# Attention weights multiplied in every slot, and the scans' preparation moved between states

## Chip, core and metric

The program runs on one core of a Trainium2 chip. The metric is device time in microseconds (us), in the median of the runs. Five engines run side by side, each through its own instructions in program order: TensorE (PE) multiplies matrices, VectorE (DVE), ScalarE (ACT) and GpSimd (POOL) work on elements, SyncE (SP) issues DMAs. They wait for each other on semaphores alone.

## What is computed

Four layers, each `x = x + layer(norm(x))` on x of 4 x 96 x 56 x 56. Two kinds of stage matter here.

Layer 0 is attention with 3 heads per image over 3136 tokens, head size 16:

```python
attn = jnp.einsum('bhnd,bhmd->bhnm', q, k) * scale
attn = jax.nn.softmax(attn, axis=-1)
out = jnp.einsum('bhnm,bhmd->bhnd', attn, v)
```

Layers 1 and 3 scan the image along 8 and 4 directions with 192 channels and 16 states each. Layer 1:

```python
delta = jax.nn.softplus(dts + dt_projs_bias[None, :, :, None])
...
hc = hc * jnp.exp(d_t[..., None] * A[None]) + (d_t * u_t)[..., None] * B_t[:, :, None, :]
return (hc, jnp.einsum('bkdn,bkn->bkd', hc, C_t))
...
y = cross_merge(ys, h, w).reshape(b, DI, L)
```

Layer 3 is the same in outline; its states are `phi * cumsum(dbx / (phi + 1e-12))` with `phi = exp(-cumsum(dA))`. Layer 2 (a window attention) is not touched.

## The kernel before

**Attention** (205 to 2171 us). There are 12 heads `g` (4 images of 3), each in 7 passes `qc` of 448 queries, each pass in 13 slots `pi` of two key tiles of 128 (the last slot has one). In slot `n`, counted through all heads, PE writes two score tiles (L373, bf16) for ACT's exponential (L469, to `Pr[n % NPR]`), and between them one or two matmuls `maximum` (L310) of the next head, whose row maxima DVE reduces (L520). The weights times values, `pv(m)` (L335), are float32 matmuls, one for each key tile, into one of four strips of 32 columns of bank 4 (`j = t % 4`). `m` runs three slots behind `n`: in every second slot `pv(m - 1)` and `pv(m)` stand together, four matmuls, and the last slot of a pass stands alone. So a pass has 7 groups of them. After a pass `combine` (L342) adds the strips up, in the next slot. `NPR` is the number of buffers `Pr`; the exponential of slot `n` waits for `pv(n - NPR)`. `prep` spreads the preparation of the next image over the middle head of each of the first three images.

**Scans.** Layer 1 runs them twice (a pair of images each, 2387 to 6431 and 6746 to 10790 us), 8 directions of 7 tiles: 56 tiles. Layer 3 runs them twice (12224 to 14843 and 15428 to 18044 us) with 4 x 7 = 28 tiles, and there `ratio` is true. A tile is 448 positions in three channel groups `c`. It has 16 states `r`; a pair of state and channel is a step `s = 3r + c`. In each state POOL forms the scans' inputs (`input1`, L1288, `Tr`) and projects (L1296, `Hc`) the channels that DVE doesn't (`ON_DVE` is 2 in layer 1, 1 in layer 3), ACT forms the decays (L1110) and in layer 3 the ratios (`weight`, L1118, a tanh), DVE scans (L1218) and projects (L1225), in layer 3 it also finishes the inputs (`input2`, L1201), and PE adds the projected states up in PSUM (`gather_n`, L991). ACT also copies the last column of each scan (`keep_psum` L1124, `keep_sbuf` L1129) to `st`, from which the same state of the next tile starts.

While tile `q` runs, tile `q + 1` is prepared. On each engine `prepare(q + 1, ...)` is called once a state (PE, DVE, POOL, SP) or once a step (ACT), and a table of numbers says which part stands where. In the order in which data goes through them: `gather` (ACT, copies `xc` to `xs`), `proj` (PE, L954), `keep_rows` and `keep_dts` (ACT, L1030, L1035), `put_rows` (SP), `pre_delta` (PE, L959) with `absolute`, `positive` and `expo` (ACT, L1042, L1046), `one_plus` and `minus_w` (ACT, L1057, L1061), `loga` (ACT, L1067), `total` (PE, L967 to L971: four matmuls into the one bank `X`, which add the softplus up), `delta` (ACT, L1071), `inputs` (L1171 on DVE in layer 1; on POOL in layer 3) and in layer 3 `one_less` and `cumsum` (DVE, L1187). `X` serves `proj`, `pre_delta` and `total` in turn, one write at a time.

A finished tile's sums go from PSUM to `yacc` in `merge` (ACT, L1101), 3 copies, and PE sets the bank to the next tile's old sums in `seed` (L1002), which waits for them.

Of the kernel before, what the change touches and what calls it, by code (L numbers as in the profile page):

```python
# [16 lines left out]
NT = L // T  # L17
# [137 lines left out]

KT = [(t * 128, min(128, L - t * 128)) for t in range(25)]
NG, NS = 3 * NI, 13 * NT
NQ, NPR = 4, 6
PREP = 8 + 2 * NT + 25


# [65 lines left out]
def attention(chip, K, D, src, dst, scr):  # L227
# [3 lines left out]
    with ExitStack() as ctx:  # L231
# [40 lines left out]
        def pe(e):  # L272
# [83 lines left out]
            last = None  # L356
            for g in range(NG):
                b, h = divmod(g, 3)
                s = g % NQ
                e.wait_ge(b7_free, B7["rows", g, 6] + 1)  # L360
                if g == 0:
                    e.wait_ge(ones, 1)
                for at in range(NS):
                    qc, pi = divmod(at, 13)
                    n = g * NS + at
                    units = list(max_units(at)) if g + 1 < NG else []
                    if n >= 2:
                        e.wait_ge(s_exp, n - 1)
                    for i, t in enumerate(slot_tiles(pi)):
                        if i and units:  # L370
                            maximum(g + 1, units.pop(0))
                        k0, kn = KT[t]
                        a = e.matmul(PS[0:kn, 2 * (n % 2) + i, 0:T], KK[s][0:99, k0:k0 + kn],  # L373
                                     Q[s][0:99, qc * T:qc * T + T], start=True, stop=True)
                    a.then_inc(s_mm, 1)
                    if last is not None:
                        combine(*last)
                        last = None
                    m = n - 3
                    if m >= 0 and m % 13 % 2 == 1:  # L380
                        pv(m - 1)
                        pv(m)
                    elif m >= 0 and m % 13 == 12:
                        pv(m)
                        last = divmod(m // 13, NT)
                    what, fq = finish_item(at)
                    if g and what == "add":
                        add(g - 1, fq)
                    for u in units:
                        maximum(g + 1, u)  # L390
                    if h == 1 and b + 1 < NI:
                        for f in prep_items(at):
                            prep(b + 1, f)
                if g + 1 < NG:
                    for i in range(7):
                        rows(g + 1, i)
# [476 lines left out]
def scans(chip, K, D, lay, pair, xc, yacc, bcd):  # L873
# [5 lines left out]
    NK, ratio = len(lay.scans), lay.ratio  # L879
# [4 lines left out]
    NQS = NK * NT  # L884
# [14 lines left out]
    with ExitStack() as ctx:  # L899
# [45 lines left out]
        def pe(e):  # L945
            def proj(q):
                k = q // NT
                e.wait_ge(xs_ready, 3 * (q + 1))
                e.wait_ge(xp_ld[k % 2], 32 * (k // 2 + 1))
                if q:  # L950
                    e.wait_ge(x_free, use(q, "proj"))
                    e.wait_ge(total_read, 3 * q)
                for c in range(3):
                    a = e.matmul(PS[0:76, XB, 0:T], xp[:, k % 2, c, :], xs[:, c, :], start=(c == 0), stop=(c == 2))  # L954
                a.then_inc(x_full, 1)

            def pre_delta(q, c):
                e.wait_ge(x_free, use(q, "delta", c))
                e.matmul(X, dw[:, q // NT % 2, c, :], dts[:], start=True, stop=True).then_inc(x_full, 1)  # L959

            def total(q, c):
                s = q % 2
                e.wait_ge(x_free, use(q, "total", c))
                e.wait_ge(minus, q + 1 if ratio else 3 * q + c + 1)
                if c:
                    e.wait_ge(total_read, 3 * q + c)
                e.matmul(X, K["ident"][:], du[:, s, c, :], start=True, stop=False)  # L967
                e.matmul(X, K["nident" if ratio else "ident"][:], w1[:, c, :], start=False, stop=False)
                e.wait_ge(logd, 3 * q + c + 1)
                e.matmul(X, K["ident"][:], logs(q)[:, c, :], start=False, stop=False)  # L970
                e.matmul(X, K["ident"][:], dl[:, s, c, :], start=False, stop=True).then_inc(x_full, 1)  # L971

            def prepare(q, r):
                if r == 1:
                    proj(q)
                elif 2 <= r < 5:
                    pre_delta(q, r - 2)
                elif 8 <= r < 11:
                    total(q, r - 8)

            def gather_n(g):

                q, nn = divmod(g, 16)
                for c in range(3):
                    if nn == 0:
                        seed(q, c)
                    if c < ON_DVE:
                        e.wait_ge(h_done, ON_DVE * g + c + 1)
                    elif c == ON_DVE:
                        e.wait_ge(hp_done, g + 1)  # L990
                    e.matmul(PS[:, YB + c, 0:T], K["ident"][:], Hc[:, g % NHC, c, :], start=False,  # L991
                             stop=(nn == 15)).then_inc(y_done, 1)

            def seed(q, c):
                k, j, order, rev, jj = tile(q)
                if q:
                    e.wait_ge(y_free, 3 * (q - 1) + c + 1)
                else:
                    e.wait_ge(y_init, 1)
                for i, p in enumerate(pieces(order, jj, w)):  # L1000
                    off, dims, ro, rd = mirrored(*p) if rev else p
                    e.matmul(view(PS[:, YB + c, :], ro, rd), K["ident"][:], view(yacc, c * n + off, dims),  # L1002
                             start=(i == 0), stop=False)

            for r in range(16):
                prepare(0, r)
            for g in range(NG):
                q, r = divmod(g, 16)
                if q + 1 < NQS:
                    prepare(q + 1, r)  # L1010
                if g:
                    gather_n(g - 1)
            gather_n(NG - 1)

        def act(e):
# [56 lines left out]

            def prepare(q, s):

                if s < 3:
                    gather(q, s)
                elif s == 6:
                    keep_rows(q)
                elif s == 7:
                    keep_dts(q)  # L1080
                elif s in (9, 12, 15):
                    absolute(q, s // 3 - 3)
                elif s in (10, 13, 16):
                    positive(q, s // 3 - 3)
                elif s in (11, 14, 17):
                    expo(q, s // 3 - 3)
                elif not ratio and 18 <= s < 21:
                    one_plus(q, s - 18)
                elif not ratio and 21 <= s < 24:
                    minus_w(q, s - 21)  # L1090
                elif not ratio and 24 <= s < 27:
                    loga(q, s - 24)
                elif s in (28, 31, 34):
                    delta(q, s // 3 - 9)

            def merge(q, c):
                k, j, order, rev, jj = tile(q)
# [36 lines left out]
                e.preload_act_table_set("natural_log_exp_and_others")  # L1134
            for s in range(48):
                prepare(0, s)
                if ratio and s == 24:
                    for c in range(3):
                        loga(0, c)
            e.wait_ge(set_up, 3 if ratio else 1)  # L1140
            made = 0
            for u in range(-2, NU):
                g, c = divmod(u, 3)
                q, r = divmod(g, 16)
                s = 3 * r + c
                if ratio and u + 2 < NU:
                    weight(u + 2)
                while made < min(u + 3, NU):
                    decay(made)
                    made += 1  # L1150
                if u < 0:
                    continue
                if c == 2:
                    keep_sbuf(g)
                if q and 3 <= s < 6:
                    merge(q - 1, s - 3)
                if q + 1 < NQS:
                    prepare(q + 1, s)
                    if ratio and s == 24:
                        for i in range(3):  # L1160
                            loga(q + 1, i)
                if c == 1:
                    keep_psum(g)
# [3 lines left out]
        def dve(e):  # L1167
# [20 lines left out]
                                     ALU.mult, ALU.add).then_inc(cs_ready, 1)  # L1188

            def prepare(q, r):  # L1190
                if ratio and r == 7:
                    one_less(q)
                if 9 <= r < 12:
                    (cumsum if ratio else inputs)(q, r - 9)

            def input2(u):
                g, c = divmod(u, 3)
# [71 lines left out]
        def pool(e):  # L1269
# [3 lines left out]
                e.tensor_tensor(du[:, s, c, :], dl[:, s, c, :], xs[:, c, :], ALU.mult).then_inc(du_ready, 1)  # L1273

            def prepare(q, r):
                if ratio and 10 <= r < 13:
                    inputs(q, r - 10)

            def input1(g):
                q = g // 16  # L1280
# [32 lines left out]
        def sp(e):  # L1313
# [33 lines left out]
            for g in range(NG):  # L1347
                q, r = divmod(g, 16)
                if q % NT == 0 and r == 0 and q // NT + 1 < NK:
                    load(q // NT + 1)  # L1350
                if q + 1 < NQS and r == 3:
                    put_rows(q + 1)
                if g + NBS - 1 < NG:
                    spread(g + NBS - 1)
# [841 lines left out]
```

## Time and profile before

| | us |
|---|---|
| median of 3 runs | 18453.19 (18451.84 to 18455.21) |
| the profiled execution | 18450.81, of it a span of 18449.0 |
| busy: DVE, PE, POOL, ACT | 15991.3, 14360.0, 12258.1, 11878.1 |
| attention (layer 0) | 205 to 2171 |
| layer 1's scans | 2387 to 6431, 6746 to 10790 |
| layer 3's scans | 12224 to 14843, 15428 to 18044 |

The span is the time between the first and last instruction on the chip in the profiled execution. An engine's busy time is over the whole span, and an engine can be the one that all others wait for in one stage and idle in the next, so the profile is read by stage. In a waiting row, the engine named behind the arrow did what ended the wait last.

### The profile page before, as it was taken

How to read it: one execution, taken by the hardware profiler on the slowest of the kernel's cores; microseconds unless marked ns; L12 is line 12 of the kernel's file. 1: busy time of each engine (PE TensorE's matmuls, PEld its weight loads, DVE VectorE, ACT ScalarE, POOL GpSimd, SP SyncE). 2: the span in 40 equal slices, each digit the busy share in tenths (PEclk: the TensorE clock that was granted, in tenths of full speed). 3: DMA queues.
4: the chain of work that ended last, by engine and by line, in shares of the span. 5: the costliest groups of instructions: out<-in, count | busy, mean ns of one | idle time of the engine just before them, and what ended most of it. 6: DMA issues, size and time to landing. Idle time of an engine off the chain costs nothing. (4 is left out here: it accounts for less than half of the span.)

```text
span 18449.0 us, 184822 instructions
## 1 busy us (share of the span) xinstructions
PE 14360.0 (78%) x39472; PEld 5978.9 (32%) x39472; DVE 15991.3 (87%) x21043; ACT 11878.1 (64%) x23997; POOL 12258.1 (66%) x5733
## 2 busy tenths in 40 slices
PE   7999878888888768888888866667777776777776
PEld 2222233333333323333333334423323332332333
DVE  6666489999999979999999987879999967999996
ACT  3555566666666646666666633358888836888882
POOL 0000089999899849999899830059988825998881
PEclk9999899999999989999999988888888888888888
DMA  1000033333333323333333320022222212222221
GB/s 27 13 17 13 21 95 103 107 105 103 102 103 103 97 81 105 105 106 103 102 103 104 102 66 16 9 65 82 81 80 79 78 33 68 82 81 80 80 79 30
DMA packets 508592, 1386.72 MB, mean 75 GB/s; under 512 B 109116, under 2 KB 157356, under 8 KB 504092
## 3 DMA queue, kind: packets, MB, share of 16 engines
q1 hardware_dynamic: 507464, 1374.90, 25.8%
q14 instruction: 813, 6.66, 0.1%
q8 instruction: 315, 5.16, 0.1%
HBM read 1301.95 MB, written 58.10 MB: 74 GB/s over the span
## 5 line engine op out<-in xcount | busy, mean ns | idle before, releaser
L1288 POOL TENSOR_TENSOR Tr<-du,BC 128x1344 f32<-128x1344 f32 x2688 | 8164.7, 3038 | 60.0 <-DVE du L1171 59.8
L991 PE MATMUL PS<-Hc,ident 128*128 128x448 f32 x16128 | 7105.1, 579 | 1272.3 <-POOL Hc L1296 1167.2
L991 PEld LDWEIGHTS PS<-Hc,ident 128*128 128x128 f32 x16128 | 3097.3, 201 | 5261.2 <-issue 2731.2
L1110 ACT ACTIVATE PS<-dl,A 128x448 f32<-128x448 f32 x5376 | 3402.4, 633 | 2086.6 <-DVE Hr L1218 1484.9
L1296 POOL TENSOR_TENSOR Hc<-Hr,BC 128x448 f32<-128x448 f32 (+1 forms) x2688 | 3899.2, 1451 | 1243.9 <-DVE Hr L1218 1138.9
L1218 DVE TENSOR_TENSOR_SCAN PS<-PS,st,Tr 128x448 f32<-128x448 f32 x3072 | 3346.9, 1134 | 265.0 <-ACT st L1124 252.6
L720 POOL MEMSET pad<- 128x348 f32 x6 | 2.3, 389 | 4043.5 <-POOLq L67 4043.5
L1225 DVE TENSOR_TENSOR Hc<-PS,BC 128x448 f32<-128x448 f32 x4480 | 2565.9, 605 | 0.8 <-PE PS L991 0.8
L1118 ACT ACTIVATE PS<-cs,lneps,A 128x448 f32<-128x448 f32 x2688 | 1939.9, 722 | 100.7 <-DVE PS L1218 96.7
L1201 DVE SCALAR_TENSOR_TENSOR PS<-PS,Tr 128x448 f32<-128x448 f32 x2688 | 1642.7, 611 | 201.2 <-ACT PS L1118 198.6
L1110 ACT ACTIVATE Ar<-dl,A 128x448 f32<-128x448 f32 x2688 | 1765.8, 657 | 0.0
L1218 DVE TENSOR_TENSOR_SCAN Hr<-PS,st,Tr 128x448 f32<-128x448 f32 x1536 | 1751.4, 1140 | 0.0
L1218 DVE TENSOR_TENSOR_SCAN Hr<-Ar,st,PS 128x448 f32<-128x448 f32 x1536 | 1743.8, 1135 | 0.0
L520 DVE TENSOR_REDUCE mx<-PS 128x1 f32<-128x448 f32 (+1 forms) x2100 | 1207.1, 619 | 567.2 <-PE PS L310 553.0
L469 ACT ACTIVATE Pr<-PS 128x896 f32<-128x896 f32 (+1 forms) x1092 | 953.6, 887 | 675.3 <-PE PS L373 671.7
L954 PE MATMUL PS<-xs,xp 128*76 128x448 f32 x1008 | 693.3, 851 | 608.6 <-ACT xs L1023 608.4
L967 PE MATMUL PS<-du,ident 128*128 128x448 f32 x1008 | 539.2, 619 | 494.1 <-DVE cs L1187 276.5
L1218 DVE TENSOR_TENSOR_SCAN PS<-Ar,st,PS 128x448 f32<-128x448 f32 x768 | 878.3, 1144 | 0.0
L310 PE MATMUL PS<-K,Q 96*128 96x448 bf16 (+1 forms) x2100 | 796.4, 386 | 89.7 <-DVE mx L520 56.0
L1129 ACT ACTIVATE st<-Hr 128x1 f32<-128x1 f32 (+1 forms) x2688 | 518.3, 193 | 412.9 <-DVE Hr L1218 406.0
L1002 PE MATMUL PS<-yacc,ident 128*128 128x448 f32 (+15 forms) x1320 | 750.5, 677 | 14.4 <-ACT yacc L1101 14.4
L373 PE MATMUL PS<-Q,K 99*128 99x448 bf16 (+1 forms) x2100 | 747.5, 370 | 9.1 <-ACT Pr L469 4.8
(240 smaller groups left out, 16743.7 us busy)
## 6 DMA issues: line engine op xcount, KB each, us to landing
BC<-bcscratch SPq DMA_DIRECT2D x5376, 224.0 KB, 3.6
zscratch<-zst SPq DMA_DIRECT2D x84, 224.0 KB, 2.0
bcscratch<-rows SPq DMA_DIRECT2D x336, 56.0 KB, 1.8
z<-zscratch SPq DMA_DIRECT2D x28, 672.0 KB, 4.5
xg<-mid SPq DMA_DIRECT2D x12, 1176.0 KB, 8.2
mid<-yo SPq DMA_DIRECT2D x56, 168.0 KB, 2.0
xr<-mid SPq DMA_DIRECT2D x8, 1176.0 KB, 10.0
Q<-part SPq DMA_DIRECT2D x72, 98.0 KB, 4.3
```

Of the source, the lines that this page charges most:

```text
L310: e.matmul(PS[0:qn, 5 + n % 2, 0:T], Q[s][0:96, q0:q0 + qn], KK[s][0:96, i * T:i * T + T], start=True, stop=True).then_inc(mx_mm, 1)
L469: e.activation(Pr[0:kn, n % NPR, 0:nt, :], PS[0:kn, 2 * (n % 2):2 * (n % 2) + nt, 0:T], ACT.Exp, scale=scale).then_inc(s_exp, 1)
L520: e.tensor_reduce(mx[0:qn, t, i:i + 1], PS[0:qn, 5 + n % 2, 0:T], AX.X, ALU.max).then_inc(mx_red, 1)
L991: e.matmul(PS[:, YB + c, 0:T], K["ident"][:], Hc[:, g % NHC, c, :], start=False, stop=(nn == 15)).then_inc(y_done, 1)
L1002: e.matmul(view(PS[:, YB + c, :], ro, rd), K["ident"][:], view(yacc, c * n + off, dims), start=(i == 0), stop=False)
L1110: e.activation(decay_at(u), dl[:, q % 2, c, :], ACT.Exp, scale=A[:, q // NT, c, nn:nn + 1]).then_inc(a_done, 1)
L1118: e.activation(PS[:, u % NW, 0:T], cs[:, q % 2, c, :], ACT.Tanh, scale=A2[:, q // NT, c, nn:nn + 1], bias=K["lneps"][:]).then_inc(w_done, 1)
L1201: e.scalar_tensor_tensor(out=p, in0=p, scalar=1.0, in1=Tr[:, g % NTR, c, :], op0=ALU.add, op1=ALU.mult).then_inc(t2_done, 1)
L1218: e.tensor_tensor_scan(state_at(g, c), decay_at(u), PS[:, u % NW, 0:T] if ratio else Tr[:, g % NTR, c, :], 0.0 if q % NT == 0 else st[:, n ...
L1225: e.tensor_tensor(Hc[:, g % NHC, c, :], state_at(g, c), BC[:, g % NBS, 1, :], ALU.mult).then_inc(h_done, 1)
L1288: e.tensor_tensor(Tr[:, g % NTR], du[:, q % 2], b, ALU.mult).then_inc(t_done, 1)
L1296: e.tensor_tensor(Hc[:, g % NHC, ON_DVE:3], Hr[:, g % NH], c_, ALU.mult).then_inc(hp_done, 1)
```

## The change

In attention, `pv` of one slot is issued in each slot, three slots behind, instead of two in every second, and `NPR` is 5 instead of 6. In the scans the table of numbers changes: `merge` goes to steps 0 to 2 and `gather` to 3 to 5 (they change places), everything from `keep_rows` to `loga` comes two to four steps later, `delta` five steps later, `proj` one state and the rest of PE's and DVE's preparation one or two states later. No instruction of the scans is added or taken away.

```diff
-NQ, NPR = 4, 6
+NQ, NPR = 4, 5
...
-                    m = n - 3
-                    if m >= 0 and m % 13 % 2 == 1:
-                        pv(m - 1)
-                        pv(m)
-                    elif m >= 0 and m % 13 == 12:
-                        pv(m)
-                        last = divmod(m // 13, NT)
+                    if n >= 3:
+                        pv(n - 3)
+                        if (n - 3) % 13 == 12:
+                            last = divmod((n - 3) // 13, NT)
...
-                if r == 1:
+                if r == 2:
                     proj(q)
-                elif 2 <= r < 5:
-                    pre_delta(q, r - 2)
-                elif 8 <= r < 11:
-                    total(q, r - 8)
+                elif 4 <= r < 7:
+                    pre_delta(q, r - 4)
+                elif 10 <= r < 13:
+                    total(q, r - 10)
...
-                if s < 3:
-                    gather(q, s)
-                elif s == 6:
+                if 3 <= s < 6:
+                    gather(q, s - 3)
+                elif s == 8:
                     keep_rows(q)
...
-                elif s in (9, 12, 15):
-                    absolute(q, s // 3 - 3)
...
+                elif s in (13, 16, 19):
+                    absolute(q, s // 3 - 4)
...
-                elif s in (28, 31, 34):
-                    delta(q, s // 3 - 9)
+                elif s in (33, 36, 39):
+                    delta(q, s // 3 - 11)
...
-                if q and 3 <= s < 6:
-                    merge(q - 1, s - 3)
+                if q and s < 3:
+                    merge(q - 1, s)
...
-                if 9 <= r < 12:
-                    (cumsum if ratio else inputs)(q, r - 9)
+                if 11 <= r < 14:
+                    (cumsum if ratio else inputs)(q, r - 11)
```

The other numbers: `keep_dts` 7 to 9; `positive` 10, 13, 16 to 14, 17, 20; `expo` 11, 14, 17 to 15, 18, 21; `one_plus` 18-20 to 22-24; `minus_w` 21-23 to 25-27; `loga` 24-26 to 28-30 (in layer 3 all three at 24, now 28); `one_less` state 7 to 8; POOL's `inputs` states 10-12 to 11-13; `put_rows` state 3 to 4.

The lines of the changed kernel stand three lower: L335 is L335 still, but L991 is L988 and L1110 is L1107.

PE in the middle of attention's first head, before and changed (`K_31` and `Q_27` are the next head's, `K_30` and `Q_26` this head's):

```order
L335 MATMUL PS<-Pr,V 32x448 x4
L310 MATMUL PS<-K_31,Q_27 128x448
L373 MATMUL PS<-Q_26,K_30 128x448
L310 MATMUL PS<-K_31,Q_27 128x448
L373 MATMUL PS<-Q_26,K_30 128x448
L310 MATMUL PS<-K_31,Q_27 128x448
L373 MATMUL PS<-Q_26,K_30 128x448
L310 MATMUL PS<-K_31,Q_27 128x448
L373 MATMUL PS<-Q_26,K_30 128x448
L335 MATMUL PS<-Pr,V 32x448 x4
```

```order
L335 MATMUL PS<-Pr,V 32x448 x2
L310 MATMUL PS<-K_31,Q_27 128x448
L373 MATMUL PS<-Q_26,K_30 128x448
L310 MATMUL PS<-K_31,Q_27 128x448
L373 MATMUL PS<-Q_26,K_30 128x448
L335 MATMUL PS<-Pr,V 32x448 x2
```

Eight bf16 matmuls stood between two groups of L335; now four do, and a group has two matmuls.

PE at the start of a tile in layer 1, before and changed:

```order
L954 MATMUL PS<-xs,xp 76x448 x3
L1002 MATMUL PS<-yacc,ident 128x448
L991 MATMUL PS<-Hc,ident 128x448
L1002 MATMUL PS<-yacc,ident 128x448
L991 MATMUL PS<-Hc,ident 128x448
L1002 MATMUL PS<-yacc,ident 128x448
L991 MATMUL PS<-Hc,ident 128x448
L959 MATMUL PS<-dts,dw 128x448
L991 MATMUL PS<-Hc,ident 128x448 x3
L959 MATMUL PS<-dts,dw 128x448
```

```order
L999 MATMUL PS<-yacc,ident 128x448
L988 MATMUL PS<-Hc,ident 128x448
L999 MATMUL PS<-yacc,ident 128x448
L988 MATMUL PS<-Hc,ident 128x448
L999 MATMUL PS<-yacc,ident 128x448
L988 MATMUL PS<-Hc,ident 128x448
L951 MATMUL PS<-xs,xp 76x448 x3
L988 MATMUL PS<-Hc,ident 128x448 x6
L956 MATMUL PS<-dts,dw 128x448
L988 MATMUL PS<-Hc,ident 128x448 x3
```

The seeds (L1002, now L999) now come ahead of `proj`, and two states' sums lie between `proj` and the first `pre_delta` (L959, now L956), where none lay.

ACT in the state of layer 1 in which the last logarithms and the first `delta` stand, before and changed:

```order
L1110 ACTIVATE PS<-dl,A 128x448
L1129 ACTIVATE st<-Hr 128x1
L1067 ACTIVATE lg<-du,one 128x448
L1110 ACTIVATE PS<-dl,A 128x448 x2
L1071 ACTIVATE dl<-PS 128x448
```

```order
L1064 ACTIVATE lg<-du,one 128x448
L1107 ACTIVATE PS<-dl,A 128x448
L1121 ACTIVATE st<-PS 128x2
L1107 ACTIVATE PS<-dl,A 128x448
L1126 ACTIVATE st<-Hr 128x1
L1107 ACTIVATE PS<-dl,A 128x448
L1068 ACTIVATE dl<-PS 128x448
```

One more step lies between the last `loga` and the first `delta`.

## Rows read from the trace of the kernel before

**Rows 1.** Stretches of the three kinds of stage; columns as the header says.
```profile
core 0: us, PE busy (x) PEld busy (x) DVE busy (x) ACT busy (x) POOL busy (x), PEclk, DMA share, GB/s
205.00:2171.00 1966.00, 1775.38 (x9025) 481.13 (x9022) 1242.51 (x2213) 1127.08 (x1470) 0.00 (x0) 0.93 0.07 12
2387.00:6431.00 4044.00, 3384.80 (x7845) 1458.42 (x7846) 3851.85 (x4645) 2746.01 (x6225) 3688.85 (x1790) 0.95 0.35 103
12224.00:14843.00 2619.00, 1895.04 (x3823) 788.63 (x3824) 2491.32 (x3242) 2194.31 (x4255) 2351.50 (x976) 0.86 0.28 80
```

**Rows 2.** Waits in attention: engine, line <- waited for, total us, times, longest.
```profile
DVE mx L520 <- PE PS L310: 530.0, 584, 9.6
...
ACT Pr L469 <- PE PS L373: 671.7, 850, 4.1
```

**Rows 3.** Timeline of PE in attention: start, us, instruction, tiles, count.
```profile
796.50 0.94 PE L335 MATMUL PS<-Pr,V 64*32 64x448 f32 x2
797.36 0.36 PE L310 MATMUL PS<-K,Q 96*128 96x448 bf16 x1
...
798.23 0.94 PE L342 MATMUL PS<-ev,comb 128*32 128x448 f32 x2
799.10 0.36 PE L310 MATMUL PS<-K,Q 96*128 96x448 bf16 x1
...
799.97 0.96 PE L335 MATMUL PS<-Pr,V 128*32 128x448 f32 x8
800.86 0.36 PE L310 MATMUL PS<-K,Q 96*128 96x448 bf16 x1
```

**Rows 4.** Timeline of ACT, same slot in two passes: an ordinary head, the last.
```profile
814.07 1.73 ACT L469 ACTIVATE Pr<-PS 128x896 f32<-128x896 f32 x2 [1.92 <-PE PS L373]
...
833.88 0.92 ACT L469 ACTIVATE Pr<-PS 128x896 f32<-128x896 f32 x1 [1.92 <-PE PS L373]
...
2070.07 2.67 ACT L469 ACTIVATE Pr<-PS 128x896 f32<-128x896 f32 x3 [0.47 <-PE PS L373]
...
2083.43 0.92 ACT L469 ACTIVATE Pr<-PS 128x896 f32<-128x896 f32 x1 [0.47 <-PE PS L373]
```

**Rows 5.** Stretches by head: one with the next image's preparation, one without, the last.
```profile
355.00:535.00 180.00, 163.01 (x790) 47.95 (x788) 122.13 (x206) 102.80 (x149) 0.00 (x0) 0.91 0.11 15
707.00:852.00 145.00, 138.22 (x723) 35.68 (x721) 105.14 (x188) 86.11 (x105) 0.00 (x0) 0.99 0.07 19
2056.00:2166.00 110.00, 107.55 (x554) 22.51 (x557) 8.42 (x15) 83.23 (x105) 0.00 (x0) 0.90 0.01 3
```

**Rows 6.** DVE's waits in layer 1's first scans, 2387 to 6431 us.
```profile
DVE PS L1218 <- ACT st L1124: 151.6, 92, 3.7
DVE du L1171 <- ACT dl L1071: 32.8, 165, 0.5
```

**Rows 7.** Timeline of layer 1, tile 37, from state 3.
```profile
5064.14 1.01 PE L959 MATMUL PS<-dts,dw 12*128 12x448 f32 x2
...
5065.25 0.64 ACT L1042 ACTIVATE du<-PS,db 128x448 f32<-128x448 f32 x1 [3.91 <-PE PS L959]
...
5066.86 0.17 ACT L1124 ACTIVATE st<-PS 128x2 f32<-128x2 f32 x1
...
5067.16 1.16 DVE L1218 TENSOR_TENSOR_SCAN PS<-PS,st,Tr 128x448 f32<-128x448 f32 x1 [3.41 <-ACT st L1124]
```

**Rows 8.** Timeline of PE in the same tile: the first two softplus totals.
```profile
5082.52 0.99 PE L967 MATMUL PS<-du,ident 128*128 128x448 f32 x2 [0.40 <-ACT w L1061]
...
5086.62 1.02 PE L970 MATMUL PS<-lg,ident 128*128 128x448 f32 x2 [2.36 <-ACT lg L1067]
...
5092.32 0.99 PE L967 MATMUL PS<-du,ident 128*128 128x448 f32 x2 [1.67 <-DVE du L1171]
```

**Rows 9.** Timeline of DVE beside it: the inputs of two channels.
```profile
5091.55 0.62 DVE L1171 TENSOR_TENSOR du<-PS,xs 128x448 f32<-128x448 f32 x1 [0.18 <-ACT dl L1071]
...
5096.55 0.62 DVE L1171 TENSOR_TENSOR du<-PS,xs 128x448 f32<-128x448 f32 x1 [0.18 <-ACT dl L1071]
```

**Rows 10.** Timeline of layer 3: second total, between two cumulative sums of DVE.
```profile
13864.51 1.14 DVE L1187 TENSOR_TENSOR_SCAN cs<-one,cs,PS 128x448 f32<-128x448 f32 x1
...
13865.80 1.83 PE L967 MATMUL PS<-du,ident 128*128 128x448 f32 x2 [5.65 <-DVE cs L1187]
...
13867.30 2.09 POOL L1296 TENSOR_TENSOR Hc<-Hr,BC 128x896 f32<-128x896 f32 x1 [1.20 <-DVE Hr L1218]
...
13872.47 1.15 DVE L1187 TENSOR_TENSOR_SCAN cs<-one,cs,PS 128x448 f32<-128x448 f32 x1 [1.59 <-ACT dl L1071]
```

**Rows 11.** The stretch of that total, by engines.
```profile
13865.80:13869.20 3.40, 3.40 (x5) 1.76 (x6) 3.40 (x5) 1.94 (x5) 2.20 (x2) 0.50 0.16 40
```

**Rows 12.** DVE's waits in layer 3's first scans, 12224 to 14843 us.
```profile
DVE PS L1201 <- ACT PS L1118: 96.5, 69, 3.1
DVE cs L1187 <- ACT dl L1071: 29.5, 27, 1.8
```

More of the change, by code:

```diff
@@ L1073, in prepare @@
             def prepare(q, s):
-                if s < 3:
-                    gather(q, s)
-                elif s == 6:
+                if 3 <= s < 6:
+                    gather(q, s - 3)
+                elif s == 8:
                     keep_rows(q)
-                elif s == 7:
+                elif s == 9:
                     keep_dts(q)
-                elif s in (9, 12, 15):
-                    absolute(q, s // 3 - 3)
[L1083 to L1092, printed above, removed]
-                elif s in (28, 31, 34):
-                    delta(q, s // 3 - 9)
+                elif s in (13, 16, 19):
+                    absolute(q, s // 3 - 4)
+                elif s in (14, 17, 20):
+                    positive(q, s // 3 - 4)
+                elif s in (15, 18, 21):
+                    expo(q, s // 3 - 5)
+                elif not ratio and 22 <= s < 25:
+                    one_plus(q, s - 22)
+                elif not ratio and 25 <= s < 28:
+                    minus_w(q, s - 25)
+                elif not ratio and 28 <= s < 31:
+                    loga(q, s - 28)
+                elif s in (33, 36, 39):
+                    delta(q, s // 3 - 11)
             def merge(q, c):
@@ L1136, in act @@
                 prepare(0, s)
-                if ratio and s == 24:
+                if ratio and s == 28:
                     for c in range(3):
@@ L1154, in act @@
                     keep_sbuf(g)
-                if q and 3 <= s < 6:
-                    merge(q - 1, s - 3)
+                if q and s < 3:
+                    merge(q - 1, s)
                 if q + 1 < NQS:
                     prepare(q + 1, s)
-                    if ratio and s == 24:
+                    if ratio and s == 28:
                         for i in range(3):
@@ L1190, in prepare @@
             def prepare(q, r):
-                if ratio and r == 7:
+                if ratio and r == 8:
                     one_less(q)
-                if 9 <= r < 12:
-                    (cumsum if ratio else inputs)(q, r - 9)
+                if 11 <= r < 14:
+                    (cumsum if ratio else inputs)(q, r - 11)
             def input2(u):
@@ L1275, in prepare @@
             def prepare(q, r):
-                if ratio and 10 <= r < 13:
-                    inputs(q, r - 10)
+                if ratio and 11 <= r < 14:
+                    inputs(q, r - 11)
             def input1(g):
@@ L1350, in sp @@
                     load(q // NT + 1)
-                if q + 1 < NQS and r == 3:
+                if q + 1 < NQS and r == 4:
                     put_rows(q + 1)
```

## Prediction, made before the run

> **What bounds the kernel now.** First the table of stretches, since the kernel has stages with different limits [rows 1]. In attention PE is busy for 1775.38 of 1966.00 us (90%), DVE and ACT for 63% and 57%: PE's instructions set the pace, with some idle time. In layer 1's scans DVE is busy for 3851.85 of 4044.00 us (95%), POOL for 91%, PE for 84%; in layer 3's DVE again (95%), POOL 90%, ACT 84%. So in the scans only what takes away or adds a wait of DVE counts. The second view is the table of waits by stage: DVE in layer 1 [rows 6], in layer 3 [rows 12], and both readers of PE in attention [rows 2]. The third is the timeline in each of the places, which shows what stood ahead of the awaited instruction.
>
> **Attention: what is added.** Work stays the same, its grouping does not. L335 is float32, so each matmul is counted twice: the order's x4 is x8 in a trace. From the start of a group of eight to the next instruction of PE 0.89 us pass (799.97 to 800.86), from the start of a group of two 0.86 (796.50 to 797.36) [rows 3]. Four key tiles go to four column strips, and evidently run beside each other; the price of a group is nearly the same for one key tile as for four. So I cost a group of two key tiles, which the trace of before doesn't show, at 0.88 us, between 0.44 (half the group of four, if time went with work) and 0.89. The two rows say that 0.88 is right. The four bf16 matmuls between two groups take 0.87 us (797.36 to 798.23), `combine` takes 0.87 (798.23 to 799.10) [rows 3].
>
> A pass of 13 slots takes 833.88 - 814.07 = 19.81 us in an ordinary head [rows 4]. PE's sum for it is 13 x 0.87 + 7 x 0.88 + 0.87 = 18.3, so 1.5 us are idle, most of them a pair of slots' turns between PE and the readers, DVE's 530.0 and ACT's 671.7 us [rows 2]. After the change a pass has 13 groups: 12 full slots of 0.87 + 0.88 = 1.75, the last of two bf16 matmuls fewer (1.5), and `combine`: 21.0 + 1.5 + 0.9 = 23.4 to 23.55. I take 23.55, +3.74 a pass: six groups cost 5.3 us, of which the idle time takes 1.5. Eight heads are ordinary: 8 x 7 x 3.74 = **+209 us**.
>
> Three heads also prepare the next image. One takes 180 us with PE idle for 17.0; an ordinary one 145 with 6.8 [rows 5]. The 42 added groups cost 42 x 0.88 = 37 us, and the 17 us can take at most 17: 20 us a head, 2.9 a pass. Three heads: **+61 us**. In the last head there are no maxima, a pass takes 2083.43 - 2070.07 = 13.36 us [rows 4] and PE is busy for 107.55 of 110 us [rows 5]. A slot's two score matmuls are (13.36 - 7 x 0.88 - 0.87) / 13 = 0.48 us; after, 12 x (0.48 + 0.88) + 1.2 + 0.87 = 18.4 to 18.5: +5.1, times 7 = **+36 us**. Together **+306**.
>
> `NPR` 5: the exponential of slot n waits for `pv(n - 5)`, which PE issues at slot n - 2. Before, with 6, it was `pv(n - 6)`. The exponential needs PE's scores of slot n, which come behind that `pv` on the same queue, so the wait is over: 0 us. The granted clock in attention is 0.93 [rows 1], so some 14% of the stretch ran at the lower level of 1.2 GHz. If denser work took all of it away, the gain is 0.07 x 1966 = 138 us; if as much again came, 138 are lost. I take none: an ordinary head stands at 0.99 already, and the others at 0.91 and 0.90 [rows 5], two rows that don't tell what denser work does.
>
> **Layer 1: what goes.** DVE waits 151.6 us in one pair's scans for `keep_psum`, in 92 waits [rows 6]. In tile 37 one is 3.41 us: ACT waited 3.91 for `pre_delta` (L959), which PE reached at 5064.14 behind the seeds and sums, did `absolute` at 5065.25, and only then `keep_psum` at 5066.86, for which the scan at 5067.16 waited [rows 7]. After the change two states' sums stand between `proj` and `pre_delta` on PE, and ACT's `absolute` comes a state and a third later behind them: it finds its bank full. The merges at steps 0 to 2 free the seeds' banks earlier, too. Some 15 us of small waits in the first states stay: -137. The waits of `inputs` (L1171) for `delta`, 32.8 us in 165 [rows 6], go: `delta` stands in the first step of the state in which its `inputs` does (33 is state 11, step 0), where before it stood in the second (28 is state 9, step 1), so ACT comes to it a step sooner. With some 2 us of them ahead of the window -35.
>
> **Layer 1: what comes.** `total` moves to states 10 to 12, `loga` to steps 28 to 30, so all logarithms are now written before the first `total` is due. Before, PE stood idle ahead of the totals in three pieces: 0.40 us for `w`, 2.36 for `lg`, 1.67 for `inputs` [rows 8], 4.43 in all. What fills PE did not change and DVE sets the pace, so the idle time stays, but as one piece, ahead of the second `total`, which waits for DVE's `inputs(0)`. What such a piece does is seen in layer 3. There PE idles 5.65 us ahead of L967 [rows 10], and the stretch behind it runs at a granted clock of 0.50, the 1.2 GHz level [rows 11]: the matmul of L967 takes 1.83 us there, and 0.99 in layer 1 [rows 8]. From one cumulative sum's end (13865.65) to the next one's start 6.82 us pass, 1.59 of them DVE's wait [rows 10]; the mean wait is 29.5 / 27 = 1.09 [rows 12], so 6.3 is usual. In layer 1 the same way has 4.20 us: from 5092.17, where one `inputs` ends, to 5096.37, where the next would start without its wait of 0.18 [rows 9]. So if the clock falls, DVE waits 6.3 - 4.2 = 2.0 us a tile at `inputs(1)` and some 0.4 at `inputs(2)`. 55 tiles x 2.4 = +132 a pair. Bounds: 0 if the idle piece stays in two, 6.82 - 4.2 = 2.6 plus 0.4 if all is as slow as the row.
>
> The Trainium skill, "TensorE: Matmul & The Clock Gate", section "HAM oscillation — how this bites in real kernels", says that a wait between two bursts of matmuls sends the clock back to its lower level and the next burst runs at half speed. By it 4.43 us in one piece cost the 132 us a pair; without it the layer gains. The trace agrees for 5.65 us [rows 11]; no row shows 4.43.
>
> Per pair -137 - 35 + 132 = -40. Both: -80. `keep_rows` may now wait for `proj`, which comes a state later and at a lower clock: +10. **-70 us**, between -344 + 10 = -334 (no fall) and +56 (2.6 + 0.4 a tile, and 5 us a pair more).
>
> **Layer 3.** `loga` in one block (three logarithms between two changes of ACT's tables) moves from step 24 to 28. DVE's 96.5 us in 69 waits for `weight` [rows 12] come of it; they move by a state and stay: 0. The wait of 29.5 for `delta` stays. `merge(1)` is now in state 0, and needs the sums of the channels that POOL projects, whose projection takes 2.09 us behind the last scan [rows 10] and PE's sum behind that: ready some 2.7 us into the state. A state takes 2619 / 448 = 5.8 us [rows 1], so step 1 is due at 1.9. ACT runs ahead of DVE by up to three decays, so of the 0.8 us little gets through: 0 to 1.0 a tile, taken 0.3 (no row shows this wait). 54 tiles x 0.3 = **+15 us** (0 to +54).
>
> **Sum.** 18450.8 (the profiled execution) + 306 - 70 + 15 = 18701.8. The median lies 2.4 us above the profiled execution: **18704 us**.
>
> **The rivals.** (a) *The clock does not fall in layer 1.* For it: 4.43 is less than 5.65, and sums of the other states lie close ahead. Against: the only row of a like size. Then DVE's waits go and nothing comes: 18704 - 264 = 18440, no change to speak of. (b) *Attention's groups fit into idle time*, the other side. DVE and ACT wait 530.0 and 671.7 us for PE [rows 2]; if the turns between the engines and not PE's sum made a slot, single groups would even them out. It decides at 0.87 + 0.88 against the mean slot of 19.81 / 13 = 1.52: a group of two key tiles would have to take under 0.65. With +0 for +306 it gives 18398, faster. Against it: [rows 3], which show 0.86 for a group of one. (c) *Attention loses clock*, as far as half to all of the 138 us above: +69 to +138, about 18800. For it: the heads with other work stand at 0.91 and 0.90; against: a fuller PE has fewer idle spells. (d) *The moved steps don't take the waits of state 3 away*, because the seeds still hold PE: -137 twice is missing, 18978. Against: two states of sums lie between.
>
> **Chances.** Forecast 0.68, (a) 0.12, (b) 0.05, (c) 0.10, (d) 0.03, and 0.02 for (a) with (b), 18134. The forecast's own bounds, layer 1 from 0.9 to 2.6 us a tile, attention 3.5 to 4.3 a pass with up to 138 us of clock gained, layer 3 to +54, give 18560 to 18820, which takes in most of (c); outside are (a), (b), (d). A measurement of this kernel tells about 0.2% (37 us) from no change. Slower 0.81, same 0.12 (which is (a)), faster 0.07.
>
> **What the changed profile would show.** Right: about 23.5 us a pass in an ordinary head, 18.5 in the last; groups of L335 of four (two tiles) at 0.88 each; L1121's wait in states 3 and 4 gone; one idle piece of over 4 us ahead of the first or second L964 of each tile of layer 1, the clock at 0.50 behind it, and L1168 waiting 2 us for `delta`. Wrong: a slot under 1.6 us; L964 at 0.99 us there; a wait of DVE in states 5 and 6.

## The result and the profile after

The changed kernel takes 18669.58 us in the median (18665.62 to 18681.43, 4 runs), the kernel before 18452.51 (18447.6 to 18455.21, 4 runs). The ratio is 1.0119 with a 95% interval of 1.0107 to 1.0131: slower by 217 us, where 251 were forecast (306 - 70 + 15).

First the stretches, for the same three stages (columns as in [rows 1]; line numbers of the changed kernel are three smaller). The profile after is that of the execution of 18681.4 us, whose span is 18679.6.

```profile
core 0: us, PE busy (x) PEld busy (x) DVE busy (x) ACT busy (x) POOL busy (x), PEclk, DMA share, GB/s
205.00:2448.00 2243.00, 2114.28 (x9024) 553.58 (x9022) 1260.70 (x2213) 1145.77 (x1470) 0.00 (x0) 0.96 0.06 10
2662.00:6677.00 4015.00, 3433.18 (x7844) 1513.45 (x7844) 3842.97 (x4645) 2741.24 (x6228) 3688.83 (x1792) 0.92 0.35 104
12433.00:15059.50 2626.50, 1878.40 (x3822) 794.76 (x3822) 2492.40 (x3243) 2192.65 (x4254) 2357.07 (x975) 0.85 0.28 79
```

Attention's granted clock rose from 0.93 to 0.96, layer 1's fell from 0.95 to 0.92. By stage, from the starts and ends of the four runs of scans in the two traces:

| | before | after | change | forecast |
|---|---|---|---|---|
| start of layer 1's first scan (attention and what follows it) | 2387.0 | 2662.2 | +275 | +306 |
| layer 1, first and second pair | 4044.4, 4044.4 | 4014.4, 4004.7 | -70 | -70 |
| layer 3, first and second pair | 2618.7, 2616.3 | 2626.6, 2626.8 | +18 | +15 |
| the rest | | | +7 | 0 |

The changes add up to +230, the difference of the two profiled executions; that of the changed kernel is 12 us above its median, so the medians differ by 217.

DVE's waits, first in layer 1's first scans, then in layer 3's, against [rows 6] and [rows 12]:

```profile
DVE du L1168 <- ACT dl L1068: 135.7, 110, 3.0
DVE PS L1215 <- ACT st L1121: 32.4, 49, 1.9
```

```profile
DVE PS L1198 <- ACT PS L1115: 97.3, 59, 3.1
DVE cs L1184 <- ACT dl L1068: 34.2, 27, 1.9
```

In layer 1 151.6 us of waits for `keep_psum` became 32.4, and 32.8 us of waits for `delta` became 135.7: a new wait of 103 us took most of the 119 that the old one gave back. The stretch itself became 30 us shorter. This is how the new one looks on PE, around the second total of a tile:

```profile
5353.13 2.42 PE L988 MATMUL PS<-Hc,ident 128*128 128x448 f32 x6
5360.01 1.22 PE L964 MATMUL PS<-du,ident 128*128 128x448 f32 x2 [4.46 <-DVE du L1168]
5361.02 1.70 PE L965 MATMUL PS<-w,ident 128*128 128x448 f32 x2
5362.51 1.68 PE L967 MATMUL PS<-lg,ident 128*128 128x448 f32 x2
5364.01 0.94 PE L968 MATMUL PS<-dl,ident 128*128 128x448 f32 x2
5364.78 2.42 PE L988 MATMUL PS<-Hc,ident 128*128 128x448 f32 x6
5367.04 0.92 PE L964 MATMUL PS<-du,ident 128*128 128x448 f32 x2
...
```

One idle piece of 4.46 us stands ahead of the total, which then takes 4.77 us (5360.01 to 5364.78); the next one, with no idle time ahead of it, has 0.92 for a matmul.

In attention, the exponentials in an ordinary head (ACT's timeline) come every 1.75 us:

```profile
909.23 0.92 ACT L466 ACTIVATE Pr<-PS 128x896 f32<-128x896 f32 x1 [0.83 <-PE PS L373]
910.98 0.92 ACT L466 ACTIVATE Pr<-PS 128x896 f32<-128x896 f32 x1 [0.83 <-PE PS L373]
912.72 0.92 ACT L466 ACTIVATE Pr<-PS 128x896 f32<-128x896 f32 x1 [0.83 <-PE PS L373]
```

and PE's timeline shows why: a group of two key tiles (x4, since each float32 matmul counts twice) and four bf16 matmuls in turn.

```profile
914.36 0.95 PE L335 MATMUL PS<-Pr,V 128*32 128x448 f32 x4
915.24 0.36 PE L310 MATMUL PS<-K,Q 96*128 96x448 bf16 x1
915.44 0.35 PE L373 MATMUL PS<-Q,K 99*128 99x448 bf16 x1
915.63 0.35 PE L310 MATMUL PS<-K,Q 96*128 96x448 bf16 x1
915.83 0.35 PE L373 MATMUL PS<-Q,K 99*128 99x448 bf16 x1
916.11 0.94 PE L335 MATMUL PS<-Pr,V 128*32 128x448 f32 x4
```

The group takes 915.24 - 914.36 = 0.88 us, as forecast for one that the trace of before did not show.

### The profile page after: what moved, and what is told of

Read it like the earlier page. It is cut to its first block and busy times, and to the rows that moved or that the text cites. A ratio compares the mean times of both kernels' runs of the same rounds, so it can differ in the third digit from the quotient of the medians.

```text
span 18679.6 us, 184823 instructions
## 1 busy us (share of the span) xinstructions
PE 14766.2 (79%) x39472; PEld 6176.3 (33%) x39472; DVE 15993.7 (86%) x21043; ACT 11884.5 (64%) x23997; POOL 12267.9 (66%) x5733
## 5 line engine op out<-in xcount | busy, mean ns | idle before, releaser
L988 PE MATMUL PS<-Hc,ident 128*128 128x448 f32 x16128 | 7245.1, 589 | 1315.9 <-POOL Hc L1293 1229.8
L988 PEld LDWEIGHTS PS<-Hc,ident 128*128 128x128 f32 x16128 | 3151.9, 204 | 5272.1 <-issue 2719.9
L1107 ACT ACTIVATE PS<-dl,A 128x448 f32<-128x448 f32 x5376 | 3399.2, 632 | 1845.9 <-DVE Hr L1215 1432.4
L1107 ACT ACTIVATE Ar<-dl,A 128x448 f32<-128x448 f32 x2688 | 1764.4, 656 | 0.0
L466 ACT ACTIVATE Pr<-PS 128x896 f32<-128x896 f32 (+1 forms) x1092 | 968.9, 888 | 917.4 <-PE PS L373 915.9
L964 PE MATMUL PS<-du,ident 128*128 128x448 f32 x1008 | 621.3, 706 | 875.2 <-DVE du L1168 483.8
L335 PE MATMUL PS<-Pr,V 128*32 128x448 f32 (+1 forms) x4200 | 1111.2, 560 | 0.0
L956 PE MATMUL PS<-dts,dw 12*128 12x448 f32 x1008 | 551.5, 628 | 354.0 <-ACT dl L1043 348.2
L999 PE MATMUL PS<-yacc,ident 128*128 128x448 f32 (+15 forms) x1320 | 768.1, 691 | 35.5 <-ACT yacc L1098 35.2
L373 PE MATMUL PS<-Q,K 99*128 99x448 bf16 (+1 forms) x2100 | 746.0, 362 | 5.9 <-ACT Q L435 3.6
```

Of the source, the lines that this page charges most:

```text
L335: a = e.matmul(PS[32 * j:32 * j + 32, 4, 0:T], V[0:kn, b % 2, t, h, :], Pr[0:kn, m % NPR, i, :], start=(t < 4), stop=(t > 20))
L466: e.activation(Pr[0:kn, n % NPR, 0:nt, :], PS[0:kn, 2 * (n % 2):2 * (n % 2) + nt, 0:T], ACT.Exp, scale=scale).then_inc(s_exp, 1)
L1107: e.activation(decay_at(u), dl[:, q % 2, c, :], ACT.Exp, scale=A[:, q // NT, c, nn:nn + 1]).then_inc(a_done, 1)
```

## Experiments

### Each half of the change alone: scans_only, attn_only

scans_only is the changed kernel with this undone, attn_only the kernel before with this done:

```diff
-NQ, NPR = 4, 6
+NQ, NPR = 4, 5
-                    m = n - 3
-                    if m >= 0 and m % 13 % 2 == 1:
-                        pv(m - 1)
-                        pv(m)
...
+                    if n >= 3:
+                        pv(n - 3)
...
```

> The changed scans with the attention of before (two slots' weights together, NPR 6). If the two parts add up, the time is that of the changed kernel without what attention lost: layer 1's first scan starts at 2662.2 us instead of 2387.0, so 18669.6 - 275 = 18394 us, 0.3% faster than before; the scans' four stretches stay at 4014, 4005, 2627 and 2627 us. Rival, that the scans gain nothing of their own: 18452. A layer 1 stretch over 4044 would say that the moved steps cost time alone.

> The scans of before with the new attention (one slot's weights in each slot, NPR 5). If the parts add up: 18452.5 + 275 = 18728 us, a pass of an ordinary head about 23.6 us, the scans at 4044 and 2617 us. Rival, that part of the loss at the start comes from elsewhere: well below 18728.

Measured: scans_only 18400.82 us (18394.54 to 18415.8), ratio 0.9976 (0.9966 to 0.9986); attn_only 18730.15 (18723.59 to 18733.6), ratio 1.0154 (1.0137 to 1.0171), both beside a median before of 18449.3. The parts add up: 18449.3 - 48.5 + 280.9 = 18681.7, 12 us or 0.06% from the 18669.6 of both together. The change is one that costs 281 us and one that gains some 49. The scans' stretches of scans_only stand at 4011.2, 4011.4, 2626.6 and 2626.8 us.

### Two key tiles in one strip: same_strip

```diff
-                    kn, j = KT[t][1], t % 4
+                    kn, j = KT[t][1], t // 2 % 4
```

with the flags of the first and last matmul of each strip set to match.

> The changed kernel, but the two key tiles of a slot go to the same strip of 32 columns (strip t // 2 % 4), so all of it is computed as before and only the place of the partial sums differs. Theory (key tiles in different strips run beside each other, so a group costs 0.88 us whether of one, two or four): now a group of two takes two times 0.88, 12 x 0.87 = 10.4 us a pass and 84 x 10.4 = 877 us in all: 19547 us. Rival (a group's price is that of changing between kinds of matmul and hardly depends on its matmuls): 18670 us.

Measured: 19418.76 us in one run, 749 more than the changed kernel. PE's timeline:

```profile
1101.10 1.69 PE L335 MATMUL PS<-Pr,V 128*32 128x448 f32 x4
1102.73 0.36 PE L310 MATMUL PS<-K,Q 96*128 96x448 bf16 x1
...
1103.59 0.94 PE L335 MATMUL PS<-Pr,V 64*32 64x448 f32 x2
1104.46 0.36 PE L310 MATMUL PS<-K,Q 96*128 96x448 bf16 x1
```

Two key tiles in one strip take 1102.73 - 1101.10 = 1.63 us, two in different strips took 0.88, one takes 0.87. So key tiles in different strips do run beside each other, and the rival falls. The expected 877 us were 17% too high: the second tile adds 0.75 us, not 0.87, and the other 0.13 is paid once a group. 12 x 0.75 x 84 = 756, against the measured 749.

### The number of weight buffers: npr6

```diff
-NQ, NPR = 4, 5
+NQ, NPR = 4, 6
```

> The changed kernel with six buffers of weights instead of five. Theory (the wait is over by the time that the scores arrive): 18669.6 us, within 10. Rival (the fifth buffer holds ACT up in places): 18640 or less, with shorter passes.

Measured: 18679.15 us (18675.05 to 18687.61), no gain. In attention ACT waits 918.6 us for L373 with six buffers, and 915.9 with five. So a sixth buffer brings nothing, and five cost nothing.

### Keeping TensorE's idle time in pieces: logs_late

On scans_only, in layer 1 alone:

```diff
-                elif not ratio and 22 <= s < 25:
-                    one_plus(q, s - 22)
-                elif not ratio and 25 <= s < 28:
-                    minus_w(q, s - 25)
-                elif not ratio and 28 <= s < 31:
-                    loga(q, s - 28)
-                elif s in (33, 36, 39):
+                elif not ratio and 24 <= s < 27:
+                    one_plus(q, s - 24)
+                elif not ratio and 27 <= s < 30:
+                    minus_w(q, s - 27)
+                elif not ratio and 30 <= s < 33:
+                    loga(q, s - 30)
+                elif s in ((33, 36, 39) if ratio else (34, 37, 40)):
```

> As the run before last (new scans, old attention), but in layer 1 one_plus, minus_w and the logarithms come two steps later (24-26, 27-29, 30-32) and delta one step later (34, 37, 40), so that PE's total again waits for w, lg and inputs in turn, as in the kernel before, shifted by two states. Theory (TensorE's idle time in one piece drops its clock, and the slow totals hold DVE up by 2.4 us a tile): the idle time ahead of L964 splits into pieces as before, the granted clock stays at 1 there, DVE's waits for delta fall from 2.4 to about 0.6 us a tile: layer 1's stretches at some 3915 us each, 18394 - 200 = 18195 us. Rival (the waits come from the steps' new places, not from the clock): the stretches stay at 4005 to 4014 or grow, 18394 or more.

Measured: 18236.58 us (18225.51 to 18254.1), ratio 0.9887 (0.9872 to 0.9902), 164 us less than scans_only. Layer 1's stretches are 3923.8 and 3941.2 us, where 3915 was expected. DVE's waits in the first of them:

```profile
DVE PS L1218 <- ACT st L1124: 39.7, 54, 2.2
DVE du L1171 <- ACT dl L1071: 32.9, 165, 0.5
```

The waits for `delta` are back at the 32.8 us of [rows 6], and PE's second total has a shorter idle piece ahead of it and runs at full speed:

```profile
5088.49 0.99 PE L967 MATMUL PS<-du,ident 128*128 128x448 f32 x2 [1.67 <-DVE du L1171]
```

Placing `one_plus`, `minus_w`, `loga` and `delta` later made the kernel faster. It fits the clock, but it also moves instructions, so it does not yet prove it.

### Work that does nothing, in the idle piece: warm, warm_early

Here no instruction of the computation moves. In `total`, ahead of the second of a tile (scans_only with these lines, warm_early's place shown; `zero` is a matrix of zeros):

```diff
                 s = q % 2
+                if c == 1 and q and not ratio:
+                    for _ in range(14):
+                        e.matmul(PS[:, YB, 0:128], zero[:], K["ident"][:, 0:128], start=False, stop=False)
                 e.wait_ge(x_free, use(q, "total", c))
...
                 if c:
                     e.wait_ge(total_read, 3 * q + c)
```

The first try, warm, had them two waits lower, just ahead of the wait for `total_read`.

> New scans, old attention, and in layer 1, from the second tile on, TensorE runs 14 matmuls of 128 columns with a zero stationary matrix (they add zero to the sums) in the idle piece of 4.5 us ahead of the second total of each tile; nothing else moves. They take some 3 us if the clock holds. Theory (clock): the granted clock in the total behind them stays at 1, its first matmul takes 0.99 us and not 1.2 to 1.8, DVE's waits for delta fall from 2.4 us a tile to under 0.4: 18394 - 54 x 2 x 2.1 = 18167 us. Rival (the wait is that of the chain DVE, PE, ACT, at any clock): no change or slower, 18394 and up.

> The same 14 zero matmuls as in the run before (new scans, old attention), now ahead of the wait for delta(0) instead of behind it, so that they start right behind the sums of state 10 and are over before the second total is due. In the run before they came 2.73 us late and took 4.75 us for 28 passes at the lower clock, and only the total behind them ran at 0.92 a matmul. Theory (clock): no idle piece of over 2 us, the total takes 3.1 us and not 4.8, DVE's waits for delta fall from 2.36 us a tile to under 0.4, layer 1's stretches from 4011 to about 3905: 18401 - 212 = 18189 us. Rival (the wait is one of the chain at any clock): the stretches stay at 4011 or grow.

warm was 69 us slower than scans_only, 18469.93 us (18455.78 to 18480.49), where 18167 were expected. The cause is its place, which PE's timeline shows:

```profile
5164.29 4.75 PE L968 MATMUL PS<-ident,zero 128*128 128x128 f32 x28 [2.73 <-ACT dl L1075]
5168.87 0.92 PE L971 MATMUL PS<-du,ident 128*128 128x448 f32 x2
```

They stood behind a wait for `delta(0)` that I had overlooked, began after 2.73 us of idle time, ran for 4.75 us and ended late. The waits of DVE for `delta` in layer 1's first stretch rose to 170.4 us. But the total behind them was at 0.92 us a matmul. In warm_early, ahead of that wait:

```profile
5155.45 3.29 PE L966 MATMUL PS<-ident,zero 128*128 128x128 f32 x28
5160.08 0.99 PE L971 MATMUL PS<-du,ident 128*128 128x448 f32 x2 [1.34 <-DVE du L1175]
5160.90 0.92 PE L972 MATMUL PS<-w,ident 128*128 128x448 f32 x2
```

The same matmuls take 3.29 us instead of 4.75, and the granted clock in the total is 1.00, the 2.4 GHz level, where the changed kernel's same stretch has 0.64 (the stretches by engines, warm_early and the changed kernel):

```profile
5160.08:5163.16 3.08, 3.08 (x8) 1.59 (x9) 3.08 (x4) 1.40 (x3) 2.49 (x3) 1.00 0.14 33
```

```profile
5360.01:5364.78 4.77, 4.77 (x8) 2.21 (x9) 4.04 (x5) 1.40 (x3) 4.16 (x3) 0.64 0.34 91
```

warm_early takes 18232.72 us (18214.08 to 18241.53), ratio 0.9884 (0.9869 to 0.9899). Its waits for `delta`:

```profile
DVE du L1175 <- ACT dl L1075: 21.9, 56, 0.6
```

21.9 us against the 132.3 of scans_only (135.7 in the changed kernel): adding 14 matmuls to each tile takes 168 us off the time, of 212 expected. The rival, that the wait is one of the chain from DVE over PE to ACT at any clock, falls: the total in that chain is 4.77 - 3.08 = 1.7 us shorter with the clock held, and no instruction of the chain was moved.

### The exchange of merge and gather: swap_back

On logs_late, `gather` at steps 0 to 2 and `merge` at 3 to 5 again, with `proj` and all the rest left late:

```diff
-                if 3 <= s < 6:
-                    gather(q, s - 3)
+                if s < 3:
+                    gather(q, s)
...
-                if q and s < 3:
-                    merge(q - 1, s)
+                if q and 3 <= s < 6:
+                    merge(q - 1, s - 3)
```

> As logs_late, but gather is back at steps 0 to 2 and merge at 3 to 5, in all four stretches. If the distance between proj and pre_delta (two states) took the waits of states 3 and 4 away, layer 1's stretches stay at 3924 to 3941 us within 20, and the 0.4 us a tile in state 2 goes; if it was the exchange of merge and gather (sums copied early, seeds free early), the waits of 2.5 us a tile come back: 4060. Layer 3: with merge in state 1 again the wait of state 2 falls from 0.28 to 0.16 us a tile, 2627 to about 2621; if its loss against the kernel before came from elsewhere, 2627 stays.

Measured: 18564.73 us in one run, layer 1's stretches 4055.8 and 4056.0 us. The waits of DVE came back in full, but not the same ones; the first stretch:

```profile
DVE Hr L1218 <- ACT PS L1110: 135.5, 54, 4.4
...
DVE PS L1218 <- ACT st L1124: 25.8, 92, 0.6
```

The wait for `keep_psum` (L1124), which the change was made for, stays away. DVE now waits for a decay (L1110), and ACT's and PE's waits in the same stretch tell why:

```profile
ACT rows L1030 <- PE PS L954: 198.5, 54, 5.4
...
ACT du L1042 <- PE PS L959: 2.1, 8, 0.6
```

```profile
PE PS L1002 <- ACT yacc L1101: 271.4, 55, 5.3
```

In the kernel before ACT stood at `absolute`, for `pre_delta`:

```profile
ACT du L1042 <- PE PS L959: 167.4, 55, 4.9
```

With two states between them that wait is gone (2.1 us), but ACT stands at `keep_rows` instead, for `proj` (198.5 us), and the decays behind it are late.

`proj` is late because PE stands idle in front of the seeds until `merge` has emptied the bank, up to 5.3 us a tile, and comes out of it slow: the next seed and sum take 1.95 and 1.67 us.

```profile
5133.09 1.95 PE L1002 MATMUL PS<-yacc,ident 128*128 128x200 f32 x4 [5.26 <-ACT yacc L1101]
5134.86 1.67 PE L991 MATMUL PS<-Hc,ident 128*128 128x448 f32 x2
```

With this in mind the kernel before is read anew. Ahead of its `proj` PE waited in every tile for `gather`, and in the tile of [rows 7] the six passes of `proj` ran at half speed, before the seeds were reached (PE's timeline; then PE's sum of such waits in the stretch, and the granted clock in that tile's `proj`):

```profile
5052.41 4.76 PE L954 MATMUL PS<-xs,xp 128*76 128x448 f32 x6 [3.85 <-ACT xs L1023]
...
5056.97 1.78 PE L1002 MATMUL PS<-yacc,ident 128*128 128x136 f32 x4
```

```profile
PE PS L954 <- ACT xs L1023: 205.0, 55, 9.9
```

```profile
5052.41:5056.90 4.49, 4.49 (x6) 1.67 (x7) 4.37 (x6) 4.37 (x12) 3.95 (x3) 0.50 0.34 104
```

In the changed kernel the same six passes take 2.48 us behind no idle time, and the waits of L951 are 37.6 us in all, those of the seeds 17.3:

```profile
5319.76 2.48 PE L951 MATMUL PS<-xs,xp 128*76 128x448 f32 x6
```

So the later `proj` and `pre_delta` gain nothing without the exchange. With `gather` first, PE idles ahead of `proj` (before) or, with `proj` moved, ahead of the seeds (swap_back). With `merge` first and `proj` a state later both are ready, nearly, as PE comes by. What the exchange would do with the old places of `proj` and `pre_delta` no run shows.

For layer 3 swap_back gives a mixed answer. In the trace DVE's waits of states 1 and 2 together fell from 0.69 to 0.56 us a tile, by about the 0.12 that was expected if `merge` in state 0 caused it (the waits themselves are longer than the expectation has them). But state 3 then waits 1.6 us, and the stretches grew from 2627 to 2665 us. With `proj` late, `merge` must come early there too; the order of before, with stretches of 2617, has 0.57 us in states 1 and 2 and hardly any wait in state 3.

### Put together: best, best2

best is logs_late, with layer 3 on the table of before and 18 zero matmuls ahead of its second total; best2 is the same with warm_early's way in layer 1. Both have the attention of before. Of best2's edit:

```diff
-                if c == 1 and q and not ratio:
-                    for _ in range(14):
+                if c == 1 and q and True:
+                    for _ in range((18 if ratio else 14)):
...
-                if r == 2:
+                p, d, t = (1, 2, 8) if ratio else (2, 4, 10)
+                if r == p:
...
```

> Old attention; in layer 1 the new table with logarithms and delta late, as in logs_late (18236.6 us); in layer 3 the table of before, with 18 zero matmuls ahead of the second total's waits from the second tile on. The table of before saves layer 3's merges in state 0 and some of the wait for delta, 9 us a stretch: 18218. If the lower clock makes DVE wait 1.05 us a tile for delta in layer 3, the zero matmuls take that away too: 18218 - 2 x 26 x 1.0 = 18166 us. Rival, that the wait has another cause: 18218, or more if the matmuls run late.

> Old attention; layer 1 as in warm_early (new table, 14 zero matmuls), layer 3 as in best (table of before, 18 zero matmuls). From the stretches measured so far: 18160.7 - 2 x 14 = 18133 us, layer 1 at 3910 to 3920 and layer 3 at 2587 a stretch. Rival, that the two layers' parts don't add up: 18160 or more.

Measured: best 18160.65 us (18149.0 to 18165.72), ratio 0.9845 (0.9831 to 0.986); best2 18141.77 (18135.1 to 18161.41), ratio 0.9836 (0.9822 to 0.9849). Both beat both kernels: best2 takes 306 us less than before and 528 less than the changed kernel. Between the two no difference is sure; best2's layer 1 stretches were 3927.0 and 3923.5, above the 3910 to 3920 that I had expected. Layer 3's stretches fell to 2587.2 and 2587.1 from 2618.7 and 2616.3. In best's trace the first matmul of a second total there takes 0.99 us, where [rows 10] has 1.83, and of the two rows of [rows 12] DVE's list of waits there has only the first left (best2, 11968 to 14556 us):

```profile
DVE PS L1224 <- ACT PS L1139: 96.6, 69, 3.1
```

## Why the prediction was right, and where it was not

**Attention, +306 forecast, +275 in the trace, +281 in attn_only alone.** The step that carried it, that a group of two key tiles costs as much as one of one or of four, held to the hundredth (0.88 us), and same_strip showed its reason. Ordinary heads went from 145 to 171.5 us, 3.79 a pass against the 3.74 worked out. Too large were the other terms: the three heads with preparation grew by 13, 16 and 19 us and not by 20 each, and two ordinary heads by 19 and not 26. What was mis-sized there is the clock term, which I had put at nothing for want of a row that told what denser work does. A head with preparation and the last head, after, against [rows 5]:

```profile
381.00:574.50 193.50, 184.78 (x790) 51.94 (x791) 123.09 (x207) 104.72 (x149) 0.00 (x0) 0.97 0.10 14
...
2306.00:2442.00 136.00, 134.96 (x552) 27.05 (x552) 8.43 (x15) 87.23 (x105) 0.00 (x0) 0.99 0.01 2
```

0.91 became 0.97 and 0.90 became 0.99. The last head grew by 26 us and not by 36, and the 10 us are those of one pass, before and after:

```profile
2102.65:2129.70 27.05, 26.19 (x86) 4.56 (x86) 4.05 (x7) 12.26 (x16) 0.00 (x0) 0.62 0.00 1
```

```profile
2369.80:2391.90 22.10, 21.95 (x86) 4.58 (x87) 4.05 (x7) 12.48 (x16) 0.00 (x0) 1.00 0.00 1
```

At a granted clock of 1.00 a pass of this head grew by 5.1 us, from 13.36 to 18.46, as worked out; this one, at 0.62 before, became 5 us shorter. A busier TensorE held its clock and gave some of the price back. Rival (b), that single groups fit into idle time, fell: no pair of slots had room for another group. Rival (c), that attention loses clock, came out the other way. That `NPR` costs nothing was right (npr6).

**Layer 1, what goes.** The size was near: 151.6 us became 32.4, -119 against -137. The reason given was half of it. I followed the wait from `absolute` to L959 and took two states of sums between `proj` and `pre_delta` for the cure (before there was one state's, with the seeds). That distance does end ACT's wait at `absolute`, in swap_back too. But one step further back on PE stood the wait for `gather` and a `proj` at half speed, which I had not followed, and in swap_back a delay of the same size reaches DVE through `keep_rows`, to which the prediction gave 10 us in all. The earlier merges, to which I gave one sentence, are as necessary as the distance. Rival (d), seeds that still hold PE up, did not come about, but swap_back is what it looks like.

**Layer 1, what comes.** The three idle pieces of 4.43 us in [rows 8] joined into one of 4.46; the clock fell behind it; DVE then waits 1.96 and 0.46 us a tile at the two inputs, 2.4 in all, where 2.0 + 0.4 were forecast. Rival (a) fell, by warm_early, which holds the clock and ends the wait. The Trainium skill ("TensorE: Matmul & The Clock Gate", section "HAM oscillation — how this bites in real kernels") says of a wait between bursts of matmuls that the next burst starts at the lower clock. The trace agrees, for 4.46 us.

**Layer 1, the sum.** That -70 came out exactly is luck in part. The two kinds of wait account for -119 + 103 = -16 us in the first pair, and its stretch fell by 30. Of the other 14, DVE's shorter busy time (3851.85 to 3842.97 us) is 9 and shorter idle pieces the rest; no term of the forecast stood for them, and their cause stays open. The upper bound of +56 does not follow from its own terms: 3.0 us in 55 tiles is 165, less 172, plus 5 a pair, about nothing.

**Layer 3.** The waits for `weight` moved and stayed (96.5 to 97.3 us). The total of +15 was near +18 but made up otherwise: `merge` in state 0 costs some 0.12 us a tile, not 0.3, and the wait for `delta`, taken to stay, grew by 0.17 a tile (29.5 to 34.2 us a stretch). The two are 8 us of the 8 and 10 by which the stretches grew; the rest was not followed further.

## To carry over

The price of column strips is that of the group, not of the key tile: fill all the strips before leaving for another kind of matmul. When steps are moved so that an engine's waits come together, ask whether that engine is TensorE: here three waits of 0.40, 2.36 and 1.67 us ahead of the totals left the clock at its upper level, and the same idle time in one piece made DVE, which sets the pace, wait 2.4 us a tile instead of 0.6. Short waits are no safeguard by themselves, though: at the start of a tile of the changed kernel PE waits 1.02 and 0.47 us close together, and the granted clock of the next 3.1 us (5311.80 to 5314.94) is 0.67. Follow a wait back until an engine is reached that was not idle before it; the first releaser need not be the cause.

## What the runs showed of the hardware

Cheap work that computes nothing pays when it holds TensorE's clock: 3.29 us of zero matmuls in an idle piece of 4.46 us brought the granted clock of the next total from 0.64 to 1.00 and took 168 us off 18401; behind 2.73 us of idle time, the same matmuls ran for 4.75 us and the kernel took 69 us more. Two float32 key tiles in different column strips take 0.88 us as a group, in the same strip 1.63. In attention PE's idle share fell from 10% to 6%, and the granted clock rose from 0.93 to 0.96: in the last head that gave back 10 of the 36 us that the added groups were to cost.
